# Attention and a product-key expert layer on one core: where the picks are added, and in which order gate parts and gate blocks come

## The reference, cut to what matters

```python
q = (x @ Wq + bq).reshape(B, S, N_HEADS, D_QUERY)          # 8 heads
s1 = einsum('bshd,nd->bshn', q1, K1); s2 = ... K2           # 64 scores each
v1, i1 = top_k(s1, 10); v2, i2 = top_k(s2, 10)
all_scores = (v1[..., :, None] + v2[..., None, :]).reshape(..., 100)
vals, best = top_k(all_scores, 10)
expert_idx = take_along_axis(all_indices, best)             # 10 of 4096 experts per head
scores = softmax(vals)
h = gelu(einsum('bsd,bshkd->bshk', x, W_down[expert_idx])) * scores
out = einsum('bshk,bshkd->bsd', h, W_up[expert_idx])
```

## Time and profile before

| | us |
|---|---|
| runs (3): median, lowest, highest | 3416.23, 3402.65, 3432.29 |
| profiled execution | 3414.61 |
| its span, first to last instruction | 3412.6 |
| TensorE busy | 3171.0 (93%) |
| VectorE busy | 2607.0 (76%) |
| ScalarE busy | 2149.4 (63%) |
| GpSimd busy | 1937.3 (57%) |
| mean granted clock of TensorE | 0.935 of full speed |

### The profile page before, as it was taken

How to read it: one execution, slowest core, us unless ns; L and a number is a source line. 1 busy time by engine, 2 the same in 40 slices (tenths; PEclk the granted TensorE clock), 3 DMA queues, 4 the chain that set the end, 5 groups by cost and what they waited for, 6 DMA issues and landing times.

```text
span 3412.6 us, 87088 instructions
## 1 busy us (share of the span) xinstructions
PE 3171.0 (93%) x31284; PEld 2723.2 (80%) x31284; DVE 2607.0 (76%) x10605; ACT 2149.4 (63%) x4475; POOL 1937.3 (57%) x1758
## 2 busy tenths in 40 slices
PE   4999999992399999999999999999999999999998
PEld 3566666651389999999888999999988888999988
DVE  5566666665888888888877888888888887888842
ACT  3444444431667777777666777777776766777772
POOL 1333333333466677676666667767666666677663
PEclk9999999996699999999999999999999999999998
DMA  2111111103333343334333334333333333343342
GB/s 67 50 56 51 43 56 56 56 25 127 130 106 110 128 135 127 127 110 130 117 109 110 110 126 137 128 125 113 122 125 109 110 109 110 118 138 129 119 134 92
DMA packets 132295, 356.58 MB, mean 104 GB/s; under 512 B 13865, under 2 KB 61609, under 8 KB 129452
## 3 DMA queue, kind: packets, MB, share of 16 engines
q1 hardware_dynamic: 131868, 351.03, 31.7%
HBM read 309.01 MB, written 25.17 MB: 98 GB/s over the span
## 4 chain that ended last, share of the span: by engine, by line
PE 67%; issue 3%; ACT 2%; POOL 1%; DVE 1%; ACTq 0%; POOLq 0%; DVEq 0%
PE b_ps_a L1231 25%; PE b_ps_h L1220 20%; PE b_ps_s L1145 12%; PE b_ps_s L1195 4%; PE b_ps_s L1205 3%; PE b_ps_m L1168 2%; ACT b_ohq L1362 1%; POOL b_hid L1048 1%; PE b_ps_m L1176 1%; ACT b_hid L1383 0%; ACT b_rid L1346 0%; PE b_ps_m L1158 0%; ACT b_gateT L1296 0%; ACT b_minus_qid L1353 0%; DVE b_idx L1578 0%
## 5 line engine op out<-in xcount | busy, mean ns | idle before, releaser
L1231 PE MATMUL b_ps_a<-b_wup,b_hid 128*128 128x256 f32 x4096 | 955.7, 379 | 0.0
L1220 PE MATMUL b_ps_h<-b_xT_hi,b_wd_split 128*128 128x256 f32 x4096 | 933.2, 312 | 21.3 <-ACT b_hid L1383 21.0
L1048 POOL TENSOR_TENSOR b_hid<-b_hid,b_gates 128x512 f32<-128x512 f32 x512 | 720.2, 1411 | 183.9 <-ACT b_hid L1383 183.6
L1231 PEld LDWEIGHTS b_ps_a<-b_wup,b_hid 128*128 128x128 f32 x4096 | 744.3, 190 | 84.0
L1220 PEld LDWEIGHTS b_ps_h<-b_xT_hi,b_wd_split 128*128 128x128 f32 x4096 | 704.3, 200 | 37.1 <-issue 26.7
L1362 ACT ACTIVATE b_ohq<-b_q_no,b_minus_qid 80x128 f16<-80x128 f16 x2048 | 648.7, 391 | 1.0
L1220 PE MATMUL b_ps_h<-b_xT_lo,b_wd_split 128*128 128x256 f32 x2048 | 597.4, 292 | 0.0
L1383 ACT ACTIVATE b_hid<-b_ps_h 128x512 f32<-128x512 f32 x512 | 304.0, 594 | 369.8 <-PE b_ps_h L1220 369.8
L1063 POOL TENSOR_TENSOR b_ohq<-b_qT 80x640 f16<-80x640 f16 (+1 forms) x416 | 516.6, 1243 | 0.0
L1145 PEld LDWEIGHTS b_ps_s<-b_ohr,b_ohq 80*128 80x128 f16 x16384 | 428.5, 97 | 51.5 <-issue 33.7
L1145 PE MATMUL b_ps_s<-b_ohr,b_ohq 80*128 80x32 f16 x16384 | 432.8, 178 | 34.2 <-issue 32.4
(11 more groups left out here) (216 smaller groups left out, 5600.3 us busy)
## 6 DMA issues: line engine op xcount, KB each, us to landing
b_wd_split<-wd_parts SPq DMA_DIRECT2D x512, 512.0 KB, 3.9
a_keysh<-a_key SPq DMA_DIRECT2D x16, 896.0 KB, 5.4
a_x<-in_x SPq DMA_DIRECT2D x16, 512.0 KB, 4.8
x_between<-a_y SPq DMA_DIRECT2D x16, 512.0 KB, 3.2
b_x<-x_between SPq DMA_DIRECT2D x32, 256.0 KB, 2.7
wd_parts<-b_wd_split SPq DMA_DIRECT2D x16, 512.0 KB, 3.0
b_x1t<-x_between SPq DMA_DIRECT2D x32, 256.0 KB, 5.4
out<-b_y SPq DMA_DIRECT2D x32, 256.0 KB, 5.6
```

Of the source, the lines that this page charges most:

```text
L1048: G.tensor_tensor(hid[:, p % 4, :, :], hid[:, p % 4, :, :], gates[:, 2 * p:2 * p + 2, :], ALU.mult).then_inc(mix_done, 1)
L1220: mm = T.matmul(hbank[p % 2][:, j * C:(j + 1) * C], a, c, start=i == 0, stop=i == len(parts) - 1)
L1231: mm = T.matmul(abank[:, t * D:(t + 1) * D], hid[:, p % 4, j, t * P:(t + 1) * P], wup[:, 2 * p + j, :], start=p == 0 and j == 0 and t == 0 ...
```

## The change

1. `sum_picks` (9 matmuls) and ScalarE's copy of its result are gone. `picked` has one number for each slot and token, and VectorE fills it by one reduce behind `product`. `turn_picks` on TensorE is 2 matmuls. The positions get an array of their own instead of sharing `picked`'s.
2. On ScalarE `keep_gate_parts` comes straight behind the last Gelu, ahead of `turn_x`. `distances` run one pair later, so that the first stands behind the Gelu of pair 1 and the last four behind the loop; `negate` goes to pair 1 and `r_numbers` to pair 2.
3. On TensorE the third gate block comes ahead of the scores and of `turn_picks`, so only the fourth stands behind them; ScalarE's copies follow that order, and so does the table of PSUM banks.

```diff
-            if b == 1 and has(m + 3):
+            if b == 2 and has(m + 3):
                 for i in range(4):
                     fills["score", m + 3, i] = len(fills)
...
-        def sum_picks(m):
-            pk = work.rearrange("p (s c t) -> p s c t", s=SLOTS, c=NPAIR)
-            rows = mbank[1][:, 0:NT * WIDE * SLOTS].rearrange("p (s c t) -> p s c t", c=WIDE, t=NT)
-            pe.wait_ge(picks_done, m + 1)
-            if m:
-                pe.wait_ge(gateT_done, m)
-            for c in range(0, NPAIR, WIDE):
-                mm = T.matmul(rows, ident16[:, :], pk[:, :, c:c + WIDE, :], start=c == 0, stop=c == NPAIR - WIDE)
-            mm.then_inc(picks_pe, 1)
...
             for t in range(NT):
-                for c in range(WIDE):
-                    mm = T.matmul(mbank[0][0:SLOTS, t * P:(t + 1) * P], picked[:, :, c, t], ident16[:, :],
-                                  start=c == 0, stop=c == WIDE - 1)
+                mm = T.matmul(mbank[0][0:SLOTS, t * P:(t + 1) * P], picked[:, t, :], ident16[:, :], start=True, stop=True)
             mm.then_inc(picked_pe, 1)
...
-            if has(m + 2):
-                sum_picks(m + 2)
             if has(m + 1):
                 gate_matrix(m + 1, 1)
+                gate_matrix(m + 1, 2)
             if has(m + 3):
                 scores(m + 3)
             if has(m + 2):
                 turn_picks(m + 2)
             if has(m + 1):
-                gate_matrix(m + 1, 2)
                 gate_matrix(m + 1, 3)
...
-                if has(m + 1):
-                    if p == 0:
+                if has(m + 1) and p:
+                    if p == 1:
+                        negate(m + 1)
+                    if p == 2:
                         r_numbers(m + 1)
-                        negate(m + 1)
-                    distances(m + 1, p)
-                    if p % 2 == 0 and p:
+                    if p == PAIRS_R - 1:
+                        keep_gate_parts(m + 1)
+                    distances(m + 1, p - 1)
+                    if p % 2 == 0:
                         near(m + 1, p // 2 - 1)
+            if has(m + 1):
+                distances(m + 1, PAIRS_R - 1)
             if has(m + 3):
                 turn_x(m + 3)
-            if has(m + 1):
-                keep_gate_parts(m + 1)
...
             if has(m + 1):
                 near(m + 1, ACT_PARTS - 1)
-            if has(m + 2):
-                turn_picks(m + 2)
             if has(m + 1):
                 keep_gates(m + 1, 1)
+                keep_gates(m + 1, 2)
             if has(m + 3):
                 scores(m + 3)
             if has(m + 1):
-                keep_gates(m + 1, 2)
                 keep_gates(m + 1, 3)
...
+        def pick(m):
+            dve.wait_ge(picks_done, m + 1)
+            if m:
+                dve.wait_ge(picked_pe, m)
+            with nc.allow_low_precision(reason="one number of each sum is not zero"):
+                V.tensor_reduce(picked[:, :, :], work.rearrange("p (s c t) -> p t s c", s=SLOTS, c=NPAIR), AX.X,
+                                ALU.add).then_inc(picked_done, 1)
...
                 product(m + 2)
+                pick(m + 2)
```

More of the change, by code:

```diff
@@ L1283, in turn_x @@
             S.copy(xT_hi[:, m % 3, :, :], xT[:, :, :]).then_inc(xT_hi_done, 1)
-        def turn_picks(m):
-            act.wait_ge(picks_pe, m + 1)
-            if m:
-                act.wait_ge(picked_pe, m)
-            S.copy(picked[:, :, :, :].rearrange("p s c t -> p (s c t)"),
-                   mbank[1][:, 0:NT * WIDE * SLOTS]).then_inc(picked_done, 1)
         def turn_gates(m):
@@ L1653, in mask @@
             if m:
-                dve.wait_ge(picks_pe, m)
+                dve.wait_ge(picked_done, m)
             dve.wait_ge(lists_done[0], 5 * (m + 1))
```

7 lines of the change are left out of this document (3 added, 4 removed).

## The result

| us | before | changed |
|---|---|---|
| median of 4 runs (lowest, highest) | 3413.86 (3402.65, 3432.29) | 3333.91 (3331.1, 3338.4) |
| profiled execution | 3414.61 | 3335.69 |
| its span | 3412.6 | 3333.9 |

A forecast was written before the change was run, and what follows sets the result against it. TensorE, busy 93%, bounds the kernel, except at the chunk's head, where ScalarE does. Terms -2.15 + 2.15 - 0.41 + 1.54 - 2.47 = -1.34 us a chunk, x 32 = -42.9 from 3414.61: 3372 us, range 3340 to 3408.

The forecast's parts named there:

- the issue waits: Gate matmul waits that nothing releases, 17.9 us in 7 pieces: left outside the sum, give or take 20 us.
- 128 in a row did not lower the clock in the chunk read: TensorE's gate matmuls: 128 in a row keep the full clock, since the scores behind them take 3.55 us.
- The change of 1.34 a chunk: All terms summed over one chunk of the second phase: -1.34 us, 32 times.
- Picks: TensorE: `sum_picks` removed, -2.15 us, offset by a new wait for `near` of some 2.1; `turn_picks` -0.41.
- VectorE's sum: One VectorE reduce over 4320 f16 elements behind the product: 4.1 to 4.6 us, TensorE not held.
- The 1.5 us left over to gate block 0: Time between VectorE's one-hots being ready, at 49.8 us, and gate block 0 wanting them at 51.3.
- Head: First `down` groups of a chunk, through the fourth, freed of ScalarE's distances: 8.44 us to 5.97, -2.47.
- Third block before the scores: 256 gate matmuls now precede the scores, so the lower clock moves there from `down`: scores +1.54 us.
- The first: Rival: the clock takes it back; scores wholly at the lower clock 3436 us, chance 0.06; milder, about 3399, 0.15.
- VectorE did not become the bound: Rival: VectorE's sum beyond 6.1 us holds gate block 0; at 9.2 us, 3471 us; chance 0.06.
- The third: Rival: head not gained, ScalarE's distances still come in the way further on; 3412 us, chance 0.06.
- The fourth: Rival: the picks' removal counts, if `near` is done before the queries; -3.5 us a chunk, 3303 us, chance 0.05.

The follow-up runs named there:

- before_23: The kernel before with parts 2 and 3 of the change, TensorE's `sum_picks` kept: 3333.38 us, ratio 0.9725.
- part 1 alone: The kernel before with only VectorE adding the picks, ScalarE's order and gate blocks as before: 3432.15 us, ratio 1.003.
- near_first: The changed kernel with ScalarE's last `near` ahead of the queries' copies: 3278.73 us, ratio 0.9582.
- split_queries: The changed kernel with ScalarE's last `near` ahead of the queries' copies, and queries in two halves around gate block 1: 3267.2 us, ratio 0.953.

## Why the prediction was wrong

The step that failed is the sentence behind the sum on the issue waits: they "fall on some chunks and not others, in any kernel, and give or take 20 us here". I had the row of them and took them as noise of 17.9 us around zero. They were a term: eight chunks of before were 3.4 to 6.6 us longer by them and the clock behind them, and the changed kernel had three of 3.4 to 3.7. The seven of the eight that lie in the row's window stood 16.9 us and cost 34, since each stall also puts the queries at the lower clock. In surplus over the ordinary chunk, the difference between the kernels is 36 us of 79, and 7 of these are a second thing put at nothing: the clock falls after 128 gate matmuls in a row in some chunks, where the prediction went by the one chunk read ("128 in a row did not lower the clock in the chunk read").

The changed kernel's share in it is the luck of a place: it gave 3334, 3382, 3382 and 3338 with 0, 32, 64 and 96 matmuls ahead. Their mean is 3359, by the ratios 1.9% or some 63 us under before; the forecast of 3372 lies among the places, and the range of 3340 to 3408 left out the ones at 0 and 96. So of the 37 us that the forecast missed, about half come with the place, and it is too low over all places as well. The change of 1.34 a chunk was sized on one ordinary chunk, and measured 1.39 there; a look at the lengths of all chunks in the trace of before would have shown the eight.

Point by point:

- *Picks.* The new wait for `near` came where it was forecast: 1.96 us, 29 times in the stretch. `turn_picks` -0.50 (-0.41). Part 1 is worth nothing, as `before_23` shows: most of the gain at `turn_picks` goes back through the clock. (The 0.14 us for the semaphore should have been 0.24 by the two times given, 2024.31 and 2024.55; the sum does not use it.)
- *VectorE's sum.* 4.65 us against 4.1 to 4.6 taken: slightly above, 1.04 ns an element beside the fixed part, where the slope of the small reduces gave 0.91. The Trainium skill's price ("VectorE: DVE Perf Modes", section "The perf-mode tier table"), 4.8 to 5.1 by my estimate, was no further off. The 1.5 us left over to gate block 0 were nearly used up by something I had costed at nothing: the compare took 3.61 instead of 2.41. The third pass of one-hots starts at 2056.29 and takes 1.22; gate block 0 starts at 2057.64. TensorE was never held, but there is no room.
- *Head.* -2.46 (-2.47); the wait for the Gelu of pair 1 is gone from TensorE's waits, and it is in all kernels without part 2 (21.8 and 30.3 us).
- *Third block before the scores.* +1.18 (+1.54), and +0.43 for the gate blocks at the lower clock, which I had left out: together 1.6.
- *Rivals.* The first is true of part 1 alone and not of the whole. VectorE did not become the bound. The third did not come, the head was gained in full. The fourth (removal counts after all) did not come by itself; `near_first` makes it so, -1.8 a chunk in the mean of 29, as the prediction's condition for it said.

Shown: that the place of TensorE's program modulo 128 matmuls moves the changed kernel between 1 and 15 long chunks, that the next chunk's weight load takes part, and, in the chunk read, that no instruction packet lands during it. Open: what besides the place decides, since chunks with the place in the same stretch go without a stall, and why `before_23`, with the drift of the kernel before, runs dry in two chunks for 0.5 us where that ran dry for 2 to 3 and in more. Open too: why 128 gate matmuls lower the clock in some chunks and not in others. No version was tried at every place, and the 3267 us of `split_queries` are at one place only.

## What to carry to other kernels

List the lengths of all iterations before one of them is read as the kernel; if some are longer with the same instructions, their surplus is a term of the sum, which an edit may keep, lose or double. Where an engine waits for nothing and the DMA share was near 1 just before, try the same kernel with a few dozen matmuls ahead: if the time moves, compare edits over several places, or move the load. And when work is taken from the busiest engine, look first at what it covered: here the removal turned into a wait of the same length, until the work waited for (`near`) was moved ahead.

## What the runs showed of the hardware

- TensorE can run out of instructions while a load takes nearly all of the DMA engines (share 0.88 to 0.95): 0.5 to 3.9 us of standing, and up to 6.8 us of chunk with the clock (81.9 against 75.1, the 24th with 64 added). It depends on the program's place with a period of 128 matmuls (times at 0 and 128 added 3334 and 3340, at 64 and 192 3382 both).
- VectorE's compare, 2.41 us in every chunk of before, took 3.61 when it began (2041.90) while a GpSimd multiply was running (2040.76, 1.27 us) and another was issued at 2041.99; a later multiply of GpSimd took 3.46 instead of 1.27. The sum took 4.65 us in all 32 chunks, and two GpSimd multiplies that began during it (2049.80) took 2.51 us together, no longer than alone. The Trainium skill, "SBUF — State Buffer", section "Terms", says that VectorE and GpSimd take turns at a shared pair of ports and that the loser blocks in full; these rows agree (+1.2 and +2.2 us).
- 256 gate matmuls of 32 columns in a row bring the clock to the 1.2 GHz level in every chunk, with TensorE busy throughout (`near_first`, scores 4.55 to 6.17 against 3.70 from the 9th chunk on). 128 in a row do so in every chunk with a pause of 2 us ahead of them in place of nine wide matmuls (part 1 alone, scores 4.95 to 5.96), and without a pause in some: in before the scores take 5.39 in the 2nd, 3rd and 26th chunk, the queries in the 29th.
